# Selective scan and an integer feed-forward in a twelve-layer decoder kernel: buffers that change places from pass to pass, B turned by transposes, delta by halves, and whole-number weights in fp32r

## The chip, the cores and the metric

The kernel runs on one core of one Trainium2 chip. The metric is the time of the device in microseconds (us), the median of several runs. A core has five engines with queues of their own: TensorE (PE in the profile, its weight loads PEld), VectorE (DVE), ScalarE (ACT), GpSimd (POOL) and SyncE (SP, which here only issues transfers). They meet on semaphores alone.

## What is computed

Twelve layers run one after the other on x, 2 sequences of 1024 positions and 256 channels. The change touches two. Layer five is a gated feed-forward whose weights are whole numbers from -127 to 127, times 1/127; xn is x after a norm over its channels:

```python
g, u = xn @ (w_gate.T * SCALE), xn @ (w_up.T * SCALE)      # 256 -> 768, SCALE = 1/127
x = x + (silu(g) * u) @ (w_down.T * SCALE)                 # 768 -> 256
```

Layer six is a selective scan over 512 inner channels and 16 states, run over each sequence forward and backward, and followed by a feed-forward that the change leaves alone:

```python
xc, z = split(xn @ in_proj_w)                 # 512 and 512
u = silu(conv4(xc))                           # causal, four taps
dt, B, C = split(u @ x_proj_w)                # 16, 16, 16
delta = softplus(dt @ dt_proj_w + dt_proj_b)  # 512
h = h * exp(delta * A) + (delta * u) * B      # at each position, 512 x 16 states
y = (sum_n h * C + u * D) * silu(z)
out = y @ out_proj_w
```

## The kernel before, in words

Each engine's program is written out stage by stage (`build`, line 3752). A stage has a method for each engine; marks (`wait_ge`) order the engines, and `Meet` (line 433), or `e.meet` within a stage, makes every engine wait for all that the others have done so far.

**Layer five** (`stages_5`, line 1478). `Dequant` turns the loaded int32 weights, 4608 columns on 128 partitions, into fp32 in place, times 1/127: VectorE two thirds, GpSimd one. `Norm` (line 241) norms 16 tiles of 128 positions on VectorE, TensorE turns them, and ScalarE copies them into `K.XNT`. After a meeting, `Swiglu` (line 1410) goes over four blocks of 512 positions. For each of six chunks of 128 hidden channels TensorE makes the gate product and the up product, two fp32 matmuls of 512 columns each, in banks of PSUM that two chunks share in turn; ScalarE takes silu of the one, VectorE multiplies by the other into `hT`. After a block's chunks TensorE makes the down product of the block before (`down`: six matmuls of 256 columns for each of 16 tiles, 96 in all), and VectorE adds it to x (`summed`), behind the six chunks of the block in its queue.

**Layer six** (`Mamba`, line 2061) makes four passes: sequence 0 and 1 forward, then, after the norm's result has been turned round (`pe_flip`), both backward. A pass has two parts.

*Preparation* (`pe_before`, `pe_delta` and their like on ScalarE and VectorE): TensorE makes the inner channels in four chunks of two halves of 512 positions; ScalarE copies them into `xp` (which lie where the states `h` lie), VectorE runs the convolution with four operations of 1024 columns for each chunk, ScalarE takes silu: `u`. TensorE multiplies `u` by x_proj for dt, B and C as rows ("6 dbc"), and again for B with positions on the partitions ("6 BT", 8 x 4 matmuls of 16 columns). VectorE splits B and C into three bf16 parts (`dve_parts`). TensorE makes delta's product, two halves of four chunks with 16 rows, ScalarE takes abs, exp(-x) and log(1+x), VectorE the maximum and the sum, then `du` = delta * u.

*Scan*: TensorE turns `du` in eight blocks (`pe_turn`), ScalarE copies them out. Then 32 states follow (k: 2 halves of the sequence by 16 states). For each, ScalarE makes a diagonal matrix of B (`Dg`) and exp(delta * A) (`dA`) for four chunks, TensorE the product with B (`pe_dB`) and a copy of C on all partitions (`pe_C`), VectorE four scans of 512 columns (`dve_h`) with two multiplications, GpSimd h * C in two operations, and TensorE sums the result over the states in PSUM (`pe_sum`, matmuls with the identity, three groups behind). Only two buffers exist for `h`, so a state's scan waits for the sum of the second state before it.

*Between two scans*: TensorE makes z for the gate (`pe_gate`, two halves of four chunks), with the last sums between them; VectorE finishes y and multiplies by silu(z); then comes the next preparation, and after delta's product the out product of the pass that ended (`pe_out`, eight tiles of four matmuls of 256 columns), which VectorE copies out ahead of the next delta. In the two backward passes a matmul more for each tile turns it back. `de` and `u` have a buffer each, so the next `u` can't be made before y has been finished. Each pass begins with `e.meet`.

Of the kernel before, what the change touches and what calls it, by code (L numbers as in the profile page):

```python
# [15 lines left out]
S = 1024  # L16
NT = 16
# [6 lines left out]
RRW = 13212  # L24
ENGINES = ("pe", "act", "dve", "pool", "sp")
# [99 lines left out]
class Heap:  # L125
# [5 lines left out]
    def take(self, dims, dt=F32, p0=0, p1=128):  # L131
        n = int(np.prod(dims))
        off = self.at
        self.at += n if dt in (F32, I32) else (n + 1) // 2
# [7 lines left out]
class Kernel:  # L142


    def __init__(self, nc, ctx, ins, out):
        self.nc, self.ctx, self.ins, self.out = nc, ctx, ins, out
        self.AR = ctx.enter_context(nc.sbuf_tensor("AR", [128, LOW], F32))
        with nc.sbuf_tensor("SC", [128, TOT - LOW], F32) as SC:
            self.SC = SC
        self.RR = ctx.enter_context(nc.sbuf_tensor("RR", [128, RRW], F32R))  # L150
# [32 lines left out]
    def view(self, off, dims, dt=F32, p0=0, p1=128):  # L183
        n = int(np.prod(dims))
        words = n if dt in (F32, I32) else n // 2
# [6 lines left out]
        if dt != F32:  # L192
            ap = ap.bitcast(dt)
# [31 lines left out]
class Weights(Stage):  # L225


    def __init__(self, K, heap, name, dt=F32):
        self.n = K.ins[name].shape[1]
        self.to, self.src, self.ready = heap.take([self.n], dt), K.ins[name], K.load(f"d_{name}")  # L230
# [1160 lines left out]
class Dequant(Stage):  # L1391


    def __init__(self, K, w):
        self.K, self.w = K, w

    def dve(self, e):
        wf = self.w.to.bitcast(F32)
        e.wait_ge(self.w.ready, "all")
        for k in (0, 2):  # L1400
            s_ = slice(1536 * k, 1536 * k + 1536)
            e.tensor_scalar(wf[:, s_], self.w.to[:, s_], 1.0 / 127.0, None, ALU.mult).then_inc(self.K.vv, ("dequant", k))

    def pool(self, e):
        s_ = slice(1536, 3072)
        e.wait_ge(self.w.ready, "all")
        e.tensor_scalar(self.w.to.bitcast(F32)[:, s_], self.w.to[:, s_], 1.0 / 127.0, None, ALU.mult).then_inc(self.K.gv, ("dequant", 1))


class Swiglu(Stage):  # L1410


    def __init__(self, K, tag, nf, wg, wu, wd):
        self.K, self.tag, self.nf, self.wg, self.wu, self.wd = K, tag, nf, wg, wu, wd
        self.hT = [K.scr.take([nf, 512]) for _ in range(2)]
        self.sg = [K.scr.take([512]) for _ in range(2)]

    def pe(self, e):
        K, tag, PS, nf = self.K, self.tag, self.K.PS, self.nf

        def down(k):
            e.wait_ge(K.vv, (tag, "h", k, nf - 1))
            for i2 in range(2):
# [3 lines left out]
                for z in range(2):  # L1427
                    i = 2 * i2 + z
                    for f in range(nf):
                        t = e.matmul(PS[:, b, 256 * z:256 * z + 256], self.hT[k % 2][:, f, 128 * i:128 * i + 128], self.wd(f),  # L1430
                                     start=f == 0, stop=f == nf - 1)
                t.then_inc(K.mm, (tag, "down", k, i2))
        for k in range(4):
            for f in range(nf):
# [2503 lines left out]
```

## Time and profile before

| | us |
|---|---|
| median of 3 runs | 6441.59 (6440.6 to 6453.47) |
| the profiled execution | 6446.8, its span 6445.0 |
| TensorE busy | 5578.4, granted clock 0.915 in the mean |
| VectorE, ScalarE, GpSimd busy | 3949.9, 2840.0, 1751.8 |

The rows further down are of this profiled execution. Times are from the start of its span. A granted clock of 1.0 is 2.4 GHz and 0.5 is 1.2 GHz; a mean between them says how long each was granted. A group of the timeline merges instructions of a kind that follow each other: its start, the time from the first's start to the last's end, engine, line, operation, operands, count, and in brackets the idle time before it with what ended it. The line is that of the helper which issues (73 matmul, 76 transpose, 79 activation, 82 tensor with tensor, 85 tensor with scalar, 88 both, 91 scan).

### The profile page before, as it was taken

The numbers are of one execution on the slowest core, as the hardware profiler recorded it, in microseconds if no ns is written. First come the engines' busy times: TensorE is split into PE (matmuls) and PEld (weight loads), VectorE is DVE, ScalarE is ACT, GpSimd is POOL, SyncE is SP. The second block draws the span as 40 slices with busy tenths as digits, with TensorE's granted clock in tenths as the row PEclk, the third lists the DMA queues.
The fourth block names the chain that finished last, engine by engine and source line by source line (L and its number), as shares of the span: only waits on it lengthen the run. The fifth ranks groups of instructions, "written<-read, shape, count | busy, mean of one in ns | idle before, by whom it ended". The sixth has DMA issues, their size and how long they took to land. (4 is left out here: it accounts for less than half of the span.)

```text
span 6445.0 us, 76892 instructions
## 1 busy us (share of the span) xinstructions
PE 5578.4 (87%) x30276; PEld 3058.1 (47%) x30292; DVE 3949.9 (61%) x6870; ACT 2840.0 (44%) x4511; POOL 1751.8 (27%) x1879
## 2 busy tenths in 40 slices
PE   7978999998968889989998989987858878899685
PEld 4434445455444545656555643336734344333354
DVE  5666776766565279787795257751267754788412
ACT  4553444443026156656563246651135545466400
POOL 2302333332032036445463122102132132311112
PEclk9998999998879979898999889988979989799898
DMA  1000000000000000000000010004400000000122
GB/s 50 1 3 1 1 1 1 1 1 20 10 18 1 11 23 1 1 1 1 1 1 1 10 40 1 1 7 166 166 23 1 1 16 13 18 1 1 42 99 85
DMA packets 47910, 135.08 MB, mean 21 GB/s; under 512 B 4822, under 2 KB 31990, under 8 KB 41534
## 3 DMA queue, kind: packets, MB, share of 16 engines
q1 hardware_dynamic: 38094, 77.67, 3.5%
q0 software_dynamic: 9456, 52.50, 2.3%
q8 instruction: 239, 3.92, 0.3%
q14 instruction: 121, 0.99, 0.1%
HBM read 99.42 MB, written 31.20 MB: 20 GB/s over the span
## 5 line engine op out<-in xcount | busy, mean ns | idle before, releaser
L73 PE MATMUL PS<-SC 128*32 128x512 f32 (+13 forms) x14832 | 2807.9, 429 | 137.7 <-ACT SC L79 61.3
L79 ACT ACTIVATE SC<-PS 128x1024 f32<-128x1024 f32 (+9 forms) x2553 | 1932.5, 782 | 2031.0 <-PE PS L73 1676.9
L73 PEld LDWEIGHTS PS<-SC 128*32 128x32 f32 (+7 forms) x14832 | 1211.6, 129 | 1468.9 <-issue 596.7
L94 DVE TENSOR_REDUCE SC<-PS 128x1 f32<-128x512 f32 (+5 forms) x2368 | 1517.1, 681 | 602.3 <-PE PS L73 589.4
L82 POOL TENSOR_TENSOR SC<-SC 128x1024 f32<-128x1024 f32 (+3 forms) x892 | 1189.9, 1344 | 1538.3 <-ACT SC L79 1319.3
L73 PE MATMUL PS<-AR 128*128 128x512 f32 (+8 forms) x4286 | 1222.5, 401 | 70.0 <-DVE SC L82 14.7
L76 PE MATMUL PS<-AR,SC 128*104 128x128 bf16 (+3 forms) x4628 | 534.6, 261 | 499.6 <-DVE SC L85 216.9
L73 PEld LDWEIGHTS PS<-AR 128*128 128x128 f32 (+4 forms) x4286 | 659.0, 178 | 511.7 <-issue 316.3
L73 PE MATMUL PS<-SC,AR 128*128 128x512 f32 (+6 forms) x1922 | 770.6, 527 | 38.5 <-ACT SC L79 13.6
L76 PEld LDWEIGHTS PS<-AR,SC 128*104 128x104 bf16 (+3 forms) x4628 | 415.3, 139 | 714.5 <-issue 414.2
L91 DVE TENSOR_TENSOR_SCAN SC<-SC,PS 128x512 f32<-128x512 f32 x512 | 610.2, 1234 | 3.0 <-ACT SC L79 3.0
L97 POOL CAST SC<-SC 128x256 bf16<-128x256 f32 (+2 forms) x696 | 264.4, 407 | 1203.5 <-DVE SC L82 656.3
L79 ACT ACTIVATE SC<-SC 128x512 f32<-128x512 f32 (+7 forms) x870 | 444.7, 563 | 275.8 <-DVE SC L85 132.1
L73 PE MATMUL PS<-AR,SC 128*128 128x256 f32 (+5 forms) x1856 | 464.3, 402 | 13.3 <-DVE SC L85 10.4
L73 PEld LDWEIGHTS PS<-SC,AR 128*128 128x128 f32 (+4 forms) x1938 | 321.6, 177 | 305.9 <-issue 232.4
L82 DVE TENSOR_TENSOR SC<-SC 128x1024 f32<-128x1024 f32 (+10 forms) x523 | 398.0, 773 | 106.2 <-ACT SC L79 92.6
L73 PE MATMUL PS<-RR 64*128 64x512 f32 (+2 forms) x2688 | 429.7, 441 | 18.8 <-DVE SC L94 18.6
L73 PEld LDWEIGHTS PS<-AR,SC 128*128 128x128 f32 (+2 forms) x1856 | 333.5, 202 | 140.5 <-issue 84.4
L82 DVE TENSOR_TENSOR SC<-PS,SC 128x256 f32<-128x256 f32 (+5 forms) x321 | 142.9, 454 | 401.7 <-PE PS L73 198.7
L97 DVE COPY SC<-PS 2x512 bf16<-2x512 bf16 (+4 forms) x397 | 207.7, 523 | 238.9 <-PE PS L76 129.4
L73 PEld LDWEIGHTS PS<-RR 64*128 64x128 f32 (+1 forms) x2688 | 240.8, 185 | 151.0 <-DVE SC L94 52.0
L79 ACT ACT_TABLE_LOAD x50 | 64.2, 1283 | 532.4 <-DVE SC L85 354.0
(73 smaller groups left out, 1990.9 us busy)
## 6 DMA issues: line engine op xcount, KB each, us to landing
xg<-AR SPq DMA_DIRECT2D x20, 512.0 KB, 5.6
SC<-in_pk11e SPq DMA_DIRECT2D x8, 1152.0 KB, 6.4
SC<-in_pk11e SPq DMA_DIRECT2D x8, 1028.0 KB, 5.1
SC<-xg SPq DMA_DIRECT2D x23, 256.0 KB, 2.9
yg<-SC SPq DMA_DIRECT2D x23, 256.0 KB, 2.2
SC<-xg SPq DMA_DIRECT2D x8, 512.0 KB, 6.1
yg<-SC SPq DMA_DIRECT2D x8, 512.0 KB, 3.3
AR<-in_pk SPq DMA_DIRECT2D x2, 1562.0 KB, 8.6
```

What stands on the lines that cost most here:

```text
L73: return Step(self.real and self.real.matmul(*a, **k))
L76: return Step(self.real and self.real.transpose(*a, **k))
L79: return Step(self.real and self.real.activation(*a, **k))
L82: return Step(self.real and self.real.tensor_tensor(*a, **k))
L91: return Step(self.real and self.real.tensor_tensor_scan(*a, **k))
L94: return Step(self.real and self.real.tensor_reduce(*a, **k))
L97: return Step(self.real and self.real.tensor_copy(*a, **k))
```

## The change

**Layer five.** `Whole` copies the weights as the whole numbers that they are into fp32r (VectorE two thirds, ScalarE one); a view of the same memory is of that type. `NormParts` keeps the turned norm as two fp32r parts, high (ScalarE) and low, what is missing from the high one (VectorE); the meeting behind it is gone. Each product is two fp32r matmuls, high and low. The hidden values are split likewise: VectorE writes the product to `full`, ScalarE the high part, VectorE the low one. 1/127 is applied by silu's scale, in the product and in the sum. `summed` of the block before moves from behind the six chunks to behind the fourth (f == 3).

**Layer six.** `u` and `de` change places from pass to pass (`ud`). `xp` moves to where `dA` lies, and its products to other banks. In passes 0 to 1 and 2 to 3 the next pass's inner channels, convolution and `u` are made ahead of and between the last sums and gates; in 1 to 2 the order stays. ScalarE copies all 64 rows of dt, B and C to `dbl`; VectorE's parts read them from there, and B with positions on the partitions comes from eight transposes of 16 rows of `dbl`. Delta's product runs half, B, half. At the start of a pass delta and `du` of the first half are made and turned first; the second half is turned in front of the first sum (p == 3). The meetings at each pass are gone.

```diff
@@ -1388,38 +1397,70 @@
-class Dequant(Stage):
...
+class NormParts(Norm):
...
+    def turned(self, e):
+        K, tag = self.K, self.tag
+        for k in range(4):
+            for c in range(2):
+                e.wait_ge(K.mm, (tag, "turn", k, c))
+                e.activation(self.hi[:, c, 512 * k:512 * k + 512], K.PS[:, 2 * k + c, :], ACT.Copy).then_inc(K.av, (tag, "hi", k, c))
+
+    def dve(self, e):
+        K, tag = self.K, self.tag
+        super().dve(e)
+        for k in range(4):
+            for c in range(2):
+                s_ = slice(512 * k, 512 * k + 512)
+                e.wait_ge(K.av, (tag, "hi", k, c))
+                e.tensor_tensor(self.lo[:, c, s_], K.PS[:, 2 * k + c, :], self.hi[:, c, s_].bitcast(F32), ALU.subtract).then_inc(K.vv, (tag, "lo", k, c))
...
+            e.tensor_copy(self.to[:, s_], self.w.to[:, s_]).then_inc(self.K.vv, ("whole", k))
...
+        e.activation(self.to[:, s_], self.w.to[:, s_], ACT.Copy).then_inc(self.K.av, ("whole", 1))
...
+            e.wait_ge(K.vv, (tag, "lo", k, nf - 1))
+            if k == 0:
+                e.wait_ge(K.vv, (x.tag, "lo", 3, 1))
...
+                        for p in range(2):
+                            t = e.matmul(PS[:, b, 256 * z:256 * z + 256], self.h[k % 2][p][:, f, 128 * i:128 * i + 128], self.wd(f),
+                                         start=f + p == 0, stop=f == nf - 1 and p == 1)
...
-                        t = e.matmul(PS[:, 2 * y + z, :], w(f, c), K.XNT[:, c, 512 * k:512 * k + 512], start=c == 0, stop=c == 1)
+                        for p, part in enumerate((x.hi, x.lo)):
+                            t = e.matmul(PS[:, 2 * y + z, :], w(f, c), part[:, c, 512 * k:512 * k + 512], start=c + p == 0, stop=c + p == 2)
...
+        def high(n):
+            k, f = divmod(n, nf)
+            if k >= 2:
+                e.wait_ge(K.mm, (tag, "down", k - 2, 1))
+            e.wait_ge(K.vv, (tag, "h", n))
+            e.activation(self.h[k % 2][0][:, f, :], self.full[n % 2], ACT.Copy).then_inc(K.av, (tag, "hi", n))
+        for n in range(4 * nf):
+            y = n % 2
             e.wait_ge(K.mm, (tag, "up", n, 0))
             if n >= 2:
-                e.wait_ge(K.vv, (tag, "h", *divmod(n - 2, self.nf)))
-            e.activation(self.sg[y], K.PS[:, 2 * y, :], ACT.Silu).then_inc(K.av, (tag, "silu", n))
+                e.wait_ge(K.vv, (tag, "h", n - 2))
+            e.activation(self.sg[y], K.PS[:, 2 * (n % nf % 2), :], ACT.Silu, scale=self.unit).then_inc(K.av, (tag, "silu", n))
+            if n > 0:
+                high(n - 1)
+        high(4 * nf - 1)
...
+        def low(n):
+            k, f = divmod(n, nf)
+            e.wait_ge(K.av, (tag, "hi", n))
+            e.tensor_tensor(self.h[k % 2][1][:, f, :], self.full[n % 2], self.h[k % 2][0][:, f, :].bitcast(F32), ALU.subtract).then_inc(K.vv, (tag, "lo", k, f))
+        for n in range(4 * nf):
+            k, f = divmod(n, nf)
+            e.wait_ge(K.mm, (tag, "up", n, 1))
+            e.wait_ge(K.av, (tag, "silu", n))
+            if n >= 2:
+                e.wait_ge(K.vv, (tag, "lo", *divmod(n - 2, nf)))
+            e.scalar_tensor_tensor(out=self.full[n % 2], in0=K.PS[:, 2 * (f % 2) + 1, :], scalar=self.unit, in1=self.sg[n % 2],
+                                   op0=ALU.mult, op1=ALU.mult).then_inc(K.vv, (tag, "h", n))
+            if n > 0:
+                low(n - 1)
+            if k > 0 and f == 3:
                 summed(k - 1)
+        low(4 * nf - 1)
         summed(3)
...
-        self.u, self.de, self.du = take([4, S]), take([4, S]), take([4, S])
+
+        self.ud, self.du = [take([4, S]) for _ in range(2)], take([4, S])
...
-        self.xp = [h.rearrange("p a b -> p (a b)")[:, 0:1027] for h in self.h]
+        self.xp = [a.rearrange("p a b -> p (a b)")[:, 0:1027] for a in self.dA]
...
+    def pe_xp(self, e, sq, c):
+
+
+        K = self.K
+        for half in range(2):
+            if c >= 2:
+                e.wait_ge(K.av, ("6 xp", sq, c - 2, half))
+            elif sq in (1, 3):
+                if c == 0 and half == 0:
+                    e.wait_ge(K.av, ("6 C", sq - 1, 31))
+                else:
+                    e.wait_ge(K.vv, ("6 h", sq - 1, 31, {(0, 1): 1, (1, 0): 2, (1, 1): 3}[c, half]))
+            self.pe_xz(e, sq, c, half, self.xp_bank(c, half)).then_inc(K.mm, ("6 xp", sq, c, half))
...
-            for c in range(4):
-                t = e.matmul(PS[:, 6, 16 * tb:16 * tb + 16], self.u[:, c, 128 * tb:128 * tb + 128], self.xpw[:, c, 32:48], start=c == 0, stop=c == 3)
...
+            t = e.transpose(K.PS[:, 6, 16 * tb:16 * tb + 16], self.dbl[32:48, 128 * tb:128 * tb + 128], K.ident[32:48, 32:48])
...
+    def pe_turn(self, e, sq, half):
+
+        K = self.K
+        e.wait_ge(K.vv, ("6 du", sq, half))
+        if half == 0:
+            e.wait_ge(K.av, ("6 BT", sq))
+        for tb in range(4 * half, 4 * half + 4):
...
-            e.meet(K.marks, ("6 pass", sq))
-            self.pe_turn(e, sq)
...
+                if p == 3:
+                    self.pe_turn(e, sq, 1)
...
+            n = sq + 1
+            if sq in (0, 2):
+                self.pe_xp(e, n, 0)
+                self.pe_last(e, sq, 61)
+                self.pe_xp(e, n, 1)
+                self.pe_last(e, sq, 62)
+                self.pe_last(e, sq, 63)
+                self.pe_xp(e, n, 2)
+                self.pe_xp(e, n, 3)
+                self.pe_gate(e, sq, 0)
+                self.pe_dbc(e, n)
+                self.pe_gate(e, sq, 1, (0, 1))
+                self.pe_dt(e, n, 0)
+                self.pe_gate(e, sq, 1, (2, 3))
+                self.pe_BT(e, n)
+                self.pe_dt(e, n, 1)
+                self.pe_out(e, sq, range(8), self.K.vv)
+                continue
             self.pe_gate(e, sq, 0)
...
-            e.meet(K.marks, ("6 pass", sq))
+            self.act_dA(e, sq, 0)
             self.act_turned(e, sq, 0)
-            self.act_spread(e, sq, 0)
+            self.act_diag(e, sq, 0)
+            self.act_C(e, sq, 0)
+            self.act_spread(e, sq, 1)
             self.act_turned(e, sq, 1)
-            self.act_spread(e, sq, 1)
...
+            if sq in (0, 2):
+                self.act_xp(e, n, 0)
+                self.act_xp(e, n, 1)
+                self.act_xp(e, n, 2)
+                self.act_u(e, n, 0)
+                self.act_xp(e, n, 3)
+                self.act_u(e, n, 1)
+                self.act_u(e, n, 2)
+                self.act_gate(e, sq, 0, (0, 1, 2))
+                self.act_u(e, n, 3)
+                self.act_gate(e, sq, 0, (3,))
+                self.act_dbl(e, n)
+                self.act_gate(e, sq, 1, (0, 1))
+                self.act_abs(e, n, 0)
+                self.act_gate(e, sq, 1, (2, 3))
+                self.act_BT(e, n)
+                self.act_abs(e, n, 1)
+                self.act_log(e, n)
+                continue
...
+            self.dve_du(e, sq, 0)
+            self.dve_delta(e, sq, 1)
             self.dve_du(e, sq, 1)
             for k in range(32):
                 self.dve_h(e, sq, k)
...
+            if sq in (0, 2):
+                self.dve_edges(e, n)
+                self.dve_conv(e, n, 0)
+                self.dve_y(e, sq, 1)
+                for c in range(1, 4):
+                    self.dve_conv(e, n, c)
+                self.dve_gated(e, sq, 0)
+                self.dve_parts(e, n)
+                self.dve_max(e, n, 0)
+                self.dve_gated(e, sq, 1)
+                self.dve_max(e, n, 1)
+                self.dve_out(e, sq, range(8), True)
+                self.dve_delta(e, n, 0)
+                continue
             self.dve_y(e, sq, 1)
```

## Rows read from the trace of the kernel before

**Rows 1.** The page, part 1: busy time and share of each engine.
```profile
PE 5578.4 (87%) x30276; PEld 3058.1 (47%) x30292; DVE 3949.9 (61%) x6870; ACT 2840.0 (44%) x4511; POOL 1751.8 (27%) x1879
```

**Rows 2.** Windows: busy time (count) per engine, then granted clock, DMA share, GB/s.
```profile
2103.70:2125.40 21.70, 8.51 (x32) 6.13 (x32) 19.02 (x58) 6.33 (x13) 4.72 (x1) 0.56 0.14 49
2125.40:2252.60 127.20, 126.34 (x384) 73.75 (x384) 22.15 (x33) 15.61 (x25) 0.00 (x0) 0.98 0.00 0
...
2268.80:2347.00 78.20, 58.18 (x162) 32.23 (x162) 40.58 (x46) 35.23 (x46) 0.00 (x0) 0.64 0.00 0
2347.00:2539.40 192.40, 186.29 (x837) 117.29 (x838) 188.19 (x195) 137.62 (x316) 147.84 (x63) 0.98 0.00 1
2539.40:2638.20 98.80, 87.10 (x269) 50.42 (x267) 51.08 (x63) 38.31 (x52) 2.35 (x1) 0.83 0.00 0
...
2831.80:2951.00 119.20, 96.97 (x332) 59.56 (x331) 64.29 (x117) 46.56 (x66) 2.34 (x1) 0.80 0.00 0
...
3143.50:3246.10 102.60, 90.59 (x285) 53.24 (x283) 54.42 (x70) 38.26 (x52) 2.35 (x1) 0.83 0.00 0
```

**Rows 3.** Groups by form, TensorE in 2125.4 to 2252.6: count, busy, mean ns.
```profile
L73 PE MATMUL PS<-AR 128*128 128x512 f32 x192 | 85.2, 605 | 0.7 <-PE PS L76 0.7
L73 PE MATMUL PS<-AR,SC 128*128 128x256 f32 x192 | 41.9, 379 | 0.0
```

**Rows 4.** Timeline, layer five: the conversion, and VectorE's part of a chunk.
```profile
2103.72 5.74 DVE L85 TENSOR_SCALAR AR<-AR 128x1536 f32<-128x1536 int32 x2
...
2103.93 4.72 POOL L85 TENSOR_SCALAR AR<-AR 128x1536 f32<-128x1536 int32 x1 [67.16 <-DVE AR L82]
2109.38 1.39 DVE L106 BATCH_NORM_STATS2 SC<-AR 128x6 f32<-128x256 f32 x4
...
2131.65 0.69 DVE L82 TENSOR_TENSOR SC<-PS,SC 128x512 f32<-128x512 f32 x1 [8.48 <-PE PS L73]
```

**Rows 5.** Timeline of TensorE in layer one: pairs of fp32r matmuls from RR.
```profile
701.84 1.20 PE L73 MATMUL PS<-RR 64*128 64x512 f32 x8
...
704.35 1.94 PE L73 MATMUL PS<-SC 128*64 128x512 f32 x8
```

**Rows 6.** Timeline of TensorE from the end of scan 0 into scan 1.
```profile
2538.34 7.13 PE L73 MATMUL PS<-AR 128*128 128x512 f32 x16 [0.83 <-DVE SC L91]
...
2583.51 10.29 PE L73 MATMUL PS<-AR,SC 128*128 128x16 f32 x64
2593.73 14.02 PE L73 MATMUL PS<-SC,AR 16*128 16x512 f32 x16
2607.67 15.87 PE L73 MATMUL PS<-AR,SC 128*128 128x256 f32 x64
2630.75 1.94 PE L76 MATMUL PS<-AR,SC 128*128 128x128 f32 x8 [7.21 <-DVE SC L82]
...
2640.92 1.16 PE L73 MATMUL PS<-SC 128*128 128x128 f32 x8 [0.86 <-ACT SC L79]
...
2646.46 3.78 PE L73 MATMUL PS<-SC,AR 128*128 128x512 f32 x4 [0.58 <-POOL SC L82]
```

**Rows 7.** Windows: delta's products, busy times as in rows 2, then granted clock.
```profile
2593.70:2607.60 13.90, 13.90 (x17) 5.16 (x16) 5.25 (x7) 5.09 (x8) 0.00 (x0) 0.50 0.00 0
```

**Rows 8.** Timeline of GpSimd and VectorE from scan 0 into scan 1.
```profile
2539.54 2.35 POOL L82 TENSOR_TENSOR SC<-SC 128x1024 f32<-128x1024 f32 x1 [0.59 <-DVE SC L91]
...
2575.73 0.81 DVE L85 TENSOR_SCALAR SC<-SC,AR 128x1024 f32<-128x1024 f32 x1
...
2576.57 3.93 DVE L88 SCALAR_TENSOR_TENSOR SC<-SC,AR 128x1024 f32<-128x1024 f32 x3
...
2623.92 9.01 DVE L82 TENSOR_TENSOR SC<-SC 128x2048 f32<-128x2048 f32 x4
...
2638.18 2.33 DVE L91 TENSOR_TENSOR_SCAN SC<-SC,PS 128x512 f32<-128x512 f32 x2 [0.97 <-ACT SC L79]
...
2653.25 2.33 DVE L91 TENSOR_TENSOR_SCAN SC<-SC,PS 128x512 f32<-128x512 f32 x2
```

**Rows 9.** Timeline of ScalarE: exp(-x) of delta, both halves.
```profile
2609.78 3.71 ACT L79 ACTIVATE SC<-SC 128x2048 f32<-128x2048 f32 x2
```

More of the change, by code:

```diff
@@ L2143, in pe_delta @@
             for half in range(2):
-                if c == 0 and sq > 0:
-                    e.wait_ge(K.av, ("6 z", sq - 1, 1, half))
-                t = e.matmul(PS[0:64, 4 + half, :], self.xpw[:, c, :], self.u[:, c, self.half(half)], start=c == 0, stop=c == 3)
+                if c == 0:
+                    e.wait_ge(K.av, ("6 xp", sq, 3, half))
+                t = e.matmul(PS[0:64, 4 + half, :], self.xpw[:, c, :], self.u(sq)[:, c, self.half(half)], start=c == 0, stop=c == 3)
                 if c == 3:
@@ L2148, in pe_delta, with pe_dt @@
                     t.then_inc(K.mm, ("6 dbc", sq, half))
-        if sq > 0:
+    def pe_dt(self, e, sq, half):
+        K = self.K
+        e.wait_ge(K.av, ("6 dbl", sq, half))
+        for c in range(4):
+            if half == 1:
+                e.wait_ge(K.vv, ("6 max", sq, 0, c))
+            elif sq in (1, 3):
+                e.wait_ge(K.av, ("6 z", sq - 1, 0, c))
+            elif sq == 2:
+                e.wait_ge(K.vv, ("6 y", 1, 1, c))
+            e.matmul(K.PS[:, c, :], self.dtw[0:16, 128 * c:128 * c + 128], self.dbl[0:16, self.half(half)], start=True,
+                     stop=True).then_inc(K.mm, ("6 dt", sq, half, c))
@@ L2154, in pe_delta @@
         t.then_inc(K.mm, ("6 BT", sq))
-        for half in range(2):
-            for c in range(4):
-                bank = c
-                if half == 1:
-                    e.wait_ge(K.vv, ("6 max", sq, 0, c))
-                else:
-                    e.wait_ge(K.av, ("6 xp", sq, 2 + c // 2, c % 2))
-                e.wait_ge(K.av, ("6 dbl", sq, half))
-                e.matmul(PS[:, bank, :], self.dtw[0:16, 128 * c:128 * c + 128], self.dbl[0:16, self.half(half)], start=True,
-                         stop=True).then_inc(K.mm, ("6 dt", sq, half, c))
@@ L2323, in act_delta, with act_log @@
+    def act_log(self, e, sq):
+        K = self.K
         for half in range(2):
[L2324 to L2328 removed]
+            d = self.de(sq)[:, :, self.half(half)]
             e.wait_ge(K.av, ("6 abs", sq, half, 3))
@@ new lines, in act @@
+            self.act_gate(e, sq, 0)
+            self.act_gate(e, sq, 1)
+            if sq == 1:
+                self.act_flip(e)
+                for c in range(4):
+                    self.act_xp(e, n, c)
+                    if c >= 1:
+                        self.act_u(e, n, c - 1)
+                self.act_u(e, n, 3)
+                self.act_dbl(e, n)
+                self.act_abs(e, n, 0)
+                self.act_BT(e, n)
+                self.act_abs(e, n, 1)
+                self.act_log(e, n)
@@ L2443, in dve_parts @@
             s_ = self.half(half)
-            src = K.PS[32:64, 4 + half, :]
-            e.wait_ge(K.mm, ("6 dbc", sq, half))
+            src = self.dbl[32:64, s_]
+            e.wait_ge(K.av, ("6 dbl", sq, half))
             if half == 1:
@@ L2556, in dve @@
         e.tensor_scalar(self.An, self.An, -1.0, None, ALU.mult).then_inc(K.vv, "6 A")
-        self.dve_before(e, 0)
-        self.dve_delta(e, 0)
-        self.dve_delta_end(e, 0)
+        self.dve_edges(e, 0)
+        for c in range(4):
+            self.dve_conv(e, 0, c)
+        self.dve_parts(e, 0)
+        self.dve_max(e, 0, 0)
+        self.dve_max(e, 0, 1)
+        self.dve_delta(e, 0, 0)
         for sq in range(self.passes):
-            e.meet(K.marks, ("6 pass", sq))
+            self.dve_du(e, sq, 0)
+            self.dve_delta(e, sq, 1)
             self.dve_du(e, sq, 1)
```

348 lines of the change are left out of this document (194 added, 154 removed).

## The prediction

> **What bounds the kernel now.** I read the page first: TensorE is busy 87% of the span, no other engine over 61% [rows 1]. That average hides that layers five and six, which the change touches, have different limits, so I cut 2103.7 to 3476.7 us into stretches by busy time [rows 2]. Layer five is two stretches: a norm of 21.7 us in which VectorE is busy 19.0 and TensorE 8.5, and 127.2 us in which TensorE is busy 126.3. There, only TensorE's work counts. Layer six is a prologue of 78.2 us, four scans of some 192.4 us, and turn-rounds of 98.8, 119.2 and 102.6 us between them. In a scan VectorE and TensorE are both at 97 to 98%; nothing of the change is in the steady loop, so I leave the scans alone. In the turn-rounds TensorE is busy 81 to 88%, at a granted clock of 0.80 to 0.83, VectorE about half: one serial chain, carried mostly by TensorE, partly at its lower clock. The timelines then give the chain step by step [rows 6 to 9].
>
> **Layer five, the matmuls.** The 127.2 us hold 192 records of 512 columns and 192 of 256 [rows 3]; the code issues 96 matmuls of each kind, so an fp32 matmul is two records. Busy time over count is 85.2/192 = 0.44 us and 41.9/192 = 0.218 us a record, a little of it start-up at the low clock; the clean pace is 0.427 and 0.213. The change doubles the matmuls (high part, low part) and makes each fp32r. The nearest rows are layer one's fp32r matmuls, 64 rows by 512 columns, in pairs on the two halves of the array: from 701.84 to 704.35 ten pairs start (eight of fp32r, two of bf16, one record a matmul), 0.251 us a pair [rows 5]. A pair is two matmuls side by side, so one fp32r matmul of 512 columns is one pass: not under 0.213 (half an fp32 record, which is two passes), not over 0.251 if 128 rows behave as 64 do. I take 0.23: 192 x 0.23 = 44.2 us (41 to 48). At 256 columns the stream is 0.107; no row has fp32r there. Eight records of 128 columns, each with its own weight load, took 1.16 us with latency [rows 6], 0.145 at most, so loads can follow each other at about that. I take 0.125: 24 us (20.5 to 28).
>
> A rule of the Trainium skill speaks against this (TensorE: Matmul & The Clock Gate, "The mechanism"): a weight load overlaps running matmuls only when its row group differs. All new matmuls use all rows, so by it each would wait for its load. That rule doesn't fit the fp32 rows, where two loads and 2 x 0.427 us of streaming make 0.853 and no more; it is rival 1.
>
> **Layer five, the waits.** VectorE gets more per hidden chunk: the product and the low part, 0.69 us each [rows 4], 1.4 us against 8 x 0.23 = 1.84 us of up-matmuls; ScalarE two operations of 0.6. They fit, TensorE stays the bound. But VectorE's sum of the block before now stands behind chunk 3, and waits for down-products that TensorE issues only after chunk 5. Chunks 4 and 5 queue behind it. Twice (blocks 1 and 2) TensorE finishes, starts the next block's gate product (0.9 us) and then waits for sum and chunk 4 (0.2+0.69+0.69): 0.8 us lost. In the last block all of sum, chunk 4, low 3, chunk 5, low 4, high 5 and low 5 stand before the last down: 4.7 us. Together 6.3. Low clock at the start costs 2.4 as now (127.2 against 192 x 0.427 + 192 x 0.213 = 123). New stretch: 44.2+24+6.3+2.4 = 77 us, gain **50** (39 to 56).
>
> The conversion: two VectorE operations of 1536 columns took 5.7 us with GpSimd's 4.7 beside them [rows 4]. The third piece goes to ScalarE, idle then. I take 1.25 each without GpSimd (an estimate: 1024 columns take 0.81 [rows 8], so 1536 some 1.2; bounds 1.25 and 2.87): 3.2 us gained (0 to 3.2). The low parts of the norm (0.69 each) let the first matmul start when two are done, about 0.7 earlier than the meeting did. Layer five: 50 + 3.2 + 0.7 = **54 us**.
>
> **Layer six, B and delta.** B's turn was 32 matmuls of 16 columns, 64 records, 10.3 us [rows 6]. Eight transposes replace it; at the low clock a transpose is 0.24 us (eight in 1.94), so 1 to 2 us; I take 1.5. It stands in the chain in all four preparations, between the products and delta. Delta's eight products took 14.0 us, 1.71 each, all at granted clock 0.50 [rows 6, 7]; at the high level they would be 0.85. Before them came B's many short matmuls, during which the clock fell.
>
> Order at the start of a pass: VectorE did delta 0, delta 1, du 0, du 1 in 9.01 us [rows 8], 2.25 each, so du 0 ended at 2630.7. Now du 0 comes second, 2.25 us sooner. But then: from du 0's end the first scan came after 7.5 us, and the third state's (2653.25) after 22.5 [rows 8]; from there on the pace is 5.88 us a state. New: four transposes' copies, diagonal, B product, multiply: first scan after 6.0. Du's second half is turned only after the fourth B product, which needs the first scans; ScalarE's four copies for it stand ahead of the copies of the last states, for which GpSimd waits, and the y sums wait for GpSimd. Worked through with the rows' durations: TensorE turns at 13.3, ScalarE done at 15.8, GpSimd 16.2 to 18.6 (2.35 an operation [rows 8]), sum of state 0 at 22.0 (low clock; 3.78 for two, [rows 6]), C, B product (2.5), multiply: third scan at 25.3; at the high clock 22.8. I take 24.8. So 2.25 is gained and 2.3 to 3.4 lost: the halves bring nothing by themselves, -0.3 to -1.
>
> **Prologue.** B saves 10.0. Delta's first half starts at the high level and gains 3.4; the second waits for VectorE's split of B and C (6 us), loses about 1.5: 11.7, less 1.2 at the start of the pass: **10.5** (8 to 15).
>
> **Pass 1 to 2** (the flip stays where it is): B 8 to 9; delta products between 0 and 5 better; the start of the pass -1: **9.5** (6 to 14).
>
> **Passes 0 to 1 and 2 to 3.** Here the next pass's products, its convolution and u move ahead of the gates and sums, since u and delta change places. The convolution (4 x 4.7 us of VectorE; three of the four operations are 3.93 [rows 8]) kept TensorE nearly idle before its last products; now gates fill that. So I add up TensorE's work from the last scan's end: it comes free 1.9 us before it, at 2537.5 (2538.34 less 0.83 idle): next x 13.7 (16 records are 7.1 with latency, 6.8 without [rows 6]), three sums 5.1, gates 13.7, dbc 6.8, delta 6.8, B 1.0 to 1.5, out 13.8: 61, end at 59. Checked against VectorE: last convolution at 25.5, last u at 26.6, needed at 28.5: 2 us of slack. ScalarE's exponential and logarithm (3.71 and about 3.9, a table load of 1.28 before each [rows 9]) end by 56, so the out product is last; then copy 0.4, delta 0 and du 0, 4.5: du 0 at 64.4 against 91.2 now (2539.45 to 2630.7). For the clock falling at the short products I add 3.5: 68. Third scan at 68+24.8 = 92.8 against 113.8: **21**, and 20.7 for 2 to 3 (17 to 26 each). Removing the meetings is contained in this: the waits that remain are on buffers.
>
> Sum: 10.5+21+9.5+20.7 = 62 in layer six (50 to 78), 54 in layer five, **116 us**. The profiled execution took 6446.8 (span 6445.0); 6331. The median of the runs is 5.2 lower: **6326**.
>
> **Rivals.** (1) Loads exposed on full rows. For: no row shows fp32r with 128 rows, and pairs ran at 0.251 rather than 0.213. Against: fp32 hides its loads. A load is about 0.107 (half of a 256-column record): 192 x 0.32 + 192 x 0.214 = 102.5 instead of 68, 34 more: 6360. The Trainium skill's rule named above would give this.
> (2) fp32r on 128 rows runs at an fp32 record's pace, 0.427 and 0.213: 123 instead of 68, and the stalls stay. Layer five gains nothing: 6381. Against: pairs of 64 rows don't show it.
> (3) The turn-rounds give less: transposes and 16-row products pull the clock down, and gates and out run slow, 6 us in each of four places: 24 more, 6350. For: during delta's products the clock stood at 0.50, and eight full transposes took 1.94 us, low-level pace [rows 6, 7]. The Trainium skill (TensorE: Matmul & The Clock Gate, "PE-mode transpose") says that the full clock doesn't engage for transposes; the trace's transposes agree. Against: four products are now followed by dense gates.
> (4) Slower: fp32r on full rows takes four passes as fp32 does, in layer five's up and down loops, 0.853 and 0.427: 192 x 1.28 = 246 instead of 68, 178 more: 6504. It decides from 0.95 us for the two together. Against: the 0.251 of a pair.
> The convolution's 2 us of slack being gone is contained in (3).
>
> **Chances.** Forecast 0.52 (own range 6300 to 6345), (1) 0.13, (2) 0.09, (3) 0.22, (4) 0.03, both gains lost 0.01. The range reaches to (3) and (1): 6298 to 6370, leaving out (2), (4) and a little below. A measurement can tell 0.2% (13 us) from nothing. Faster 0.96, within 0.01, slower 0.03.
>
> **What would show it.** Layer five's TensorE stretch: one record a matmul, 192 of each width, spaced 0.23 and 0.125, in 77 us; idle of 0.8, 0.8 and 4.7 us behind VectorE. No 64-record group of 16 columns. From last scan to first scan 74 us instead of 98.8 (0 to 1), about 78 (2 to 3); the step to the third state longer than 8.3 us, behind GpSimd. If records are 0.427 apart, (2); if the gates run at half clock, (3). What would make it wrong at once: a wait of TensorE on VectorE in the middle of the turn-round.

## The result, and the profile after

The changed kernel takes 6334.59 us (median of 4 runs, 6333.54 to 6335.71), the kernel before 6444.14 (4 runs beside them, 6440.6 to 6453.47). The ratio is 0.9832, with a 95% interval of 0.982 to 0.9844: 1.7% faster. The forecast was 6326, 8.6 us too low and inside the range of 6298 to 6370. About 5 of the 8.6 is in the sum of the gains, which is 111.1 us of span (6445.0 less 6333.9) instead of 116. The rest is my step from the profiled execution to the median, since the profiled execution of after (6335.7) stands 1.1 above its median, not 5.2.

The page, part 1, of the kernel after. It answers to [rows 1]: TensorE has lost 107 us of busy time, 208 matmul records net, and the other engines little.

```profile
PE 5471.7 (86%) x30068; PEld 3002.4 (47%) x30068; DVE 3959.9 (63%) x6902; ACT 2852.2 (45%) x4536; POOL 1745.4 (28%) x1878
```

Windows of the kernel after, columns as in [rows 2]: conversion and norm of layer five, its matmuls, the prologue of layer six, then the turn-rounds 0 to 1, 1 to 2, 2 to 3.

```profile
2104.00:2122.00 18.00, 8.56 (x35) 6.20 (x33) 17.20 (x62) 7.22 (x13) 0.00 (x0) 0.60 0.17 59
2122.00:2199.90 77.90, 72.11 (x385) 61.94 (x384) 39.58 (x62) 29.39 (x50) 0.00 (x0) 0.94 0.00 1
2216.00:2278.40 62.40, 40.51 (x96) 17.59 (x97) 39.80 (x46) 37.94 (x53) 0.00 (x0) 0.72 0.00 0
2475.40:2548.50 73.10, 67.03 (x199) 35.66 (x198) 50.42 (x60) 41.12 (x59) 2.36 (x1) 0.93 0.00 0
2742.40:2850.80 108.40, 86.43 (x264) 49.78 (x264) 63.56 (x117) 49.40 (x73) 2.34 (x1) 0.80 0.00 0
3046.20:3128.20 82.00, 75.75 (x215) 40.94 (x214) 53.84 (x71) 41.16 (x59) 2.36 (x1) 0.88 0.00 1
```

Against [rows 2], layer five's matmuls take 77.9 us instead of 127.2, at the same number of records. The turn-rounds take 73.1, 108.4 and 82.0 instead of 98.8, 119.2 and 102.6, and in the first and the third the granted clock is up from 0.83 to 0.93 and 0.88. In the middle one, which is not mixed, it stayed at 0.80.

I cut both executions at the same events: start of the conversion, start of the norm that ends layer five, end of a pass's last scan, first scan of the third state of the next. From there to its last scan a pass took 178.5 us in every kernel of this study.

| part, us saved | forecast | measured |
|---|---|---|
| layer five | 54 | 54.0 |
| layer six, prologue | 10.5 | 11.4 |
| turn-round 0 to 1 | 21 | 25.3 |
| turn-round 1 to 2 | 9.5 | 7.9 |
| turn-round 2 to 3 | 20.7 | 17.0 |
| outside these parts | 0 | -4.5 |
| sum | 116 | 111.1 |

Of the -4.5, 1.3 lie ahead of layer five and 3.2 behind the last scan of layer six.

In layer five, the timeline of TensorE in the kernel after (columns: start, duration, engine and operation, count, idle before it with what released it):

```profile
2121.96 23.82 PE L74 MATMUL PS<-QB,QA 128*128 128x512 f32 x96
2145.62 5.84 PE L74 MATMUL PS<-QA,QB 128*128 128x256 f32 x48
2151.30 1.09 PE L74 MATMUL PS<-QB,QA 128*128 128x512 f32 x4
2152.84 10.53 PE L74 MATMUL PS<-QB,QA 128*128 128x512 f32 x44 [0.45 <-DVE SC L89]
...
2180.81 5.84 PE L74 MATMUL PS<-QA,QB 128*128 128x256 f32 x48
2190.81 8.37 PE L74 MATMUL PS<-QA,QB 128*128 128x256 f32 x48 [4.16 <-DVE QB L83]
```

An fp32r matmul is one record, 48 of 256 columns pass in 5.84 us, and TensorE waits for VectorE where the prediction said so: 0.45 after the next block's gate product (twice), 4.16 before the last down-products. After that wait the same 48 records need 8.37 us, at a granted clock of 0.68.

In the turn-round 0 to 1, the timeline of TensorE in the kernel after, against [rows 6]:

```profile
2485.28 13.90 PE L74 MATMUL PS<-AR 128*128 128x512 f32 x32
2499.11 7.08 PE L74 MATMUL PS<-SC,AR 128*64 128x512 f32 x16
2506.12 3.70 PE L74 MATMUL PS<-AR 128*128 128x512 f32 x8
2509.75 3.69 PE L74 MATMUL PS<-SC,AR 16*128 16x512 f32 x8
2513.38 5.40 PE L74 MATMUL PS<-AR 128*128 128x512 f32 x8
...
2519.52 3.16 PE L74 MATMUL PS<-SC,AR 16*128 16x512 f32 x7
2522.61 14.08 PE L74 MATMUL PS<-AR,SC 128*128 128x256 f32 x64
2541.73 1.97 PE L77 MATMUL PS<-AR,SC 128*128 128x128 f32 x8 [5.04 <-DVE SC L83]
```

No wait is left from the last sums to the end of the out product, the next pass's last products and the gates (the 32 records of 512 from AR, half of them each, and twice 8 more of gates) fill the time of the convolution, and delta's 16 records (3.69 and about 3.9 us) run near 0.45 us each instead of 0.88. B's eight transposes, and the first of delta's second eight records, lie in the 0.8 us left out between 2518.71 and 2519.52.

### The profile page after: what moved, and what is told of

It is laid out like the page before. It is cut to its first block and busy times, and to the rows that moved or that the text cites. A ratio compares the mean times of both kernels' runs of the same rounds, so it can differ in the third digit from the quotient of the medians.

```text
span 6333.9 us, 76568 instructions
## 1 busy us (share of the span) xinstructions
PE 5471.7 (86%) x30068; PEld 3002.4 (47%) x30068; DVE 3959.9 (63%) x6902; ACT 2852.2 (45%) x4536; POOL 1745.4 (28%) x1878
## 5 line engine op out<-in xcount | busy, mean ns | idle before, releaser
L74 PE MATMUL PS<-AR 128*128 128x128 f32 (+6 forms) x4094 | 1145.9, 393 | 68.5 <-DVE SC L83 14.8
L77 PE MATMUL PS<-AR,SC 128*104 128x128 bf16 (+2 forms) x4660 | 534.7, 260 | 485.3 <-DVE SC L86 213.1
L74 PEld LDWEIGHTS PS<-AR 128*128 128x128 f32 (+2 forms) x4094 | 624.7, 178 | 468.7 <-issue 276.3
L74 PE MATMUL PS<-SC,AR 128*128 128x512 f32 (+7 forms) x1938 | 755.4, 513 | 48.0 <-DVE SC L83 13.3
L77 PEld LDWEIGHTS PS<-AR,SC 128*104 128x104 bf16 (+2 forms) x4660 | 415.8, 138 | 700.8 <-issue 372.9
L74 PE MATMUL PS<-AR,SC 128*128 128x256 f32 (+4 forms) x1408 | 378.0, 419 | 13.3 <-DVE SC L86 10.4
L83 DVE TENSOR_TENSOR SC<-PS,SC 128x256 f32<-128x256 f32 (+3 forms) x289 | 120.7, 427 | 330.5 <-ACT SC L80 191.0
L74 PEld LDWEIGHTS PS<-AR,SC 128*128 128x128 f32 (+2 forms) x1408 | 254.5, 192 | 128.8 <-issue 79.4
```

What stands on the lines that cost most here:

```text
L74: return Step(self.real and self.real.matmul(*a, **k))
L77: return Step(self.real and self.real.transpose(*a, **k))
L83: return Step(self.real and self.real.tensor_tensor(*a, **k))
```

## The experiments

All are edits of the kernel after, but for l5_alone, which has only layer five's part of the change, and l6_alone, which has only layer six's. Numbers in brackets are 95% intervals of the ratio to the kernel before; for the kernel after it is 0.9832 (0.982 to 0.9844).

### The two halves of the change

```diff
 (l5_alone)  class Mamba: of the kernel before; Dequant, Swiglu, stages of layer five: of after
 (l6_alone)  class Mamba: of the kernel after; Dequant, Swiglu, stages of layer five: of before
```

(The classes that allot the memory are those of after in both.)

> The kernel before with layer five's change alone. My theory: the gains of the two layers are independent, and layer five's is what TensorE saves in its own stretch: 148.9 us (2103.72 to 2252.59) become 95, with up products 0.233 us apart and down products 0.12, so 54 us less than before, some 6390, while layer six stays as in before (78, 98.8, 119.2, 102.6 between scans). Rival: part of the 111 us comes or goes elsewhere (the changed kernel's layers outside five and six together are 4.5 us longer than in the profile before): then this one's time differs from before by less than 50 or more than 58 us although its layer five takes 95.

> The changed kernel with layer five as before. My theory: layer six alone gives 61 to 62 us (11.4, 25.3, 7.9 and 17.0 from the end of the scan or norm before to the third state of each pass): 6382. Rival: with layer five as before, the clock or the memory traffic at the start of layer six is another, and the prologue gives less than 8 or more than 15 us; or the sum of this gain and layer five's is not that of the changed kernel, by over 5 us.

Measured: l5_alone 6393.76 us, 0.9924 (0.9907 to 0.994); l6_alone 6392.52, 0.9918 (0.9901 to 0.9934). In l5_alone layer five took 93.05 us against 148.86, a little better than the 94.87 in after. In l6_alone the parts of layer six came out as in after, to 0.5 us (prologue to the third scan 97.4 against 96.9, turn-rounds 88.5, 125.4 and 100.5). So neither half needs the other for its gain. But unchanged code didn't keep its time: in l5_alone, whose layer six is that of before, the turn-rounds to the third state took 112.4, 137.3 and 116.5 us against 113.8, 133.2 and 117.5, so the middle one alone was 4.0 longer. And l6_alone's time missed its expectation by 10 us, and these lie behind layer six, where its instructions are those of both other kernels: from the last scan on it took 3015.7 us, before 3005.5, after 3008.7. By the medians the two halves gave 51.5 and 52.8 us, 104.3 together, where the whole change gave 109.6: 5.3 short, just past the 5 us that I had named as the rival's sign. The profile puts most of the difference behind layer six (3015.7 against 3008.7 us), not into the layers that were changed. One place of this kind, TensorE in the layer after six, first the kernel after, then the kernel before:

```profile
3388.42 30.64 PE L74 MATMUL PS<-AR 128*128 128x512 f32 x64 [10.83 <-POOL AR L83]
```

```profile
3502.76 29.12 PE L73 MATMUL PS<-AR 128*128 128x512 f32 x64 [10.65 <-POOL AR L82]
```

The same 64 records after nearly the same wait take 1.5 us more, at a granted clock of 0.90 against 0.95 in the windows of these two stretches. From the last scan to the end the kernels of this study took 3002.8 to 3015.7 us, and they came to the start of layer five between 2101.9 and 2110.1 us; I can't predict the sign of either. The -4.5 of the table is of this kind.

### The order of the turn-rounds

```diff
-            if sq in (0, 2):        # xp, u and convolution ahead of gates and sums (PE, ACT, DVE)
+            if False:
...
-            if sq == 1:
-                self.pe_flip(e)
+            if sq < 3:
+                if sq == 1:
+                    self.pe_flip(e)
```

(The waits on buffers, and the gates' banks, follow the order of 1 to 2.)

> The changed kernel without the mixing in passes 0 to 1 and 2 to 3: gates and sums first, then the next preparation, as in 1 to 2; transposes, changed buffers and delta by halves stay. My theory: the serial chain comes back, in which TensorE idles during the convolution. From the last scan to du's first half: 91.2 before, less 9.3 for B's turn, 2.3 for the order of du, 0 to 5 for a better clock: 75 to 80 against 66 in the changed kernel, so 9 to 14 us more in each of the two, 6353 to 6362. Rival: the mixing is worth little because TensorE's work alone fills the time; less than 4 us each, 6342 or less. Then the gain of 25 and 17 us would be that of the transposes and the clock.

Measured: 6356.14 us, 0.9862 (0.9843 to 0.9882), 21.6 over the kernel after, inside the expected 6353 to 6362. Its two parts were not inside theirs, 9 to 14 each: the turn-round 0 to 1 took 16.2 us more to the third state, 2 to 3 took 5.0 more. That the sum fits is in part luck. To the first scan they took 13.0 and 8.2 us more; the step from the second state to the third then added 3.2 in the one and took back 3.2 in the other. TensorE in 0 to 1, last scan at 2472.2:

```profile
2490.97 14.00 PE L74 MATMUL PS<-AR 128*128 128x512 f32 x32 [0.69 <-ACT SC L80]
2506.59 3.62 PE L74 MATMUL PS<-SC,AR 128*64 128x512 f32 x8 [1.62 <-ACT SC L80]
...
2515.38 4.27 PE L74 MATMUL PS<-SC,AR 128*64 128x512 f32 x9 [2.75 <-ACT SC L80]
...
2523.55 7.19 PE L74 MATMUL PS<-SC,AR 16*128 16x512 f32 x8 [2.60 <-DVE SC L86]
2530.66 15.94 PE L74 MATMUL PS<-AR,SC 128*128 128x256 f32 x64
```

The waits are back (0.69, 1.62, 0.49, 2.75 and 2.60 us of them), and the eight second delta products behind the last of them run at 0.90 us each, for 7.19 us, where the mixed order has 0.45. Mixing gives both the filled waits and a good part of the clock.

### B's turn

```diff
         for tb in range(8):
-            t = e.transpose(K.PS[:, 6, 16 * tb:16 * tb + 16], self.dbl[32:48, 128 * tb:128 * tb + 128], K.ident[32:48, 32:48])
+            for c in range(4):
+                t = e.matmul(K.PS[:, 6, 16 * tb:16 * tb + 16], self.u(sq)[:, c, 128 * tb:128 * tb + 128], self.xpw[:, c, 32:48], start=c == 0, stop=c == 3)
```

> The changed kernel with B's turn made again by 32 matmuls of 16 columns in place of eight transposes, at the same place. My theory: it stands in TensorE's chain in all four preparations and each pays 7 us (64 records 0.11 apart at the full clock) to 10 (at the half), less about 1.0 for the transposes: 6 to 9 each, 24 to 37 in all, 6359 to 6372. Rival 1: in the mixed preparations it hides behind ScalarE or VectorE: only two of the four pay, 12 to 18 us, 6347 to 6353. Rival 2: its short products also pull the clock down for what follows (delta's second half 1.71 apart rather than 0.85, the first out tiles slow): 5 us more for each, 45 us and more.

Measured: 6389.07 us, 0.9914 (0.9894 to 0.9933), 54.5 over the kernel after. My expectation fell and the rival's held. To the third state the four preparations took 10.8, 19.8, 15.4 and 11.8 us more: 57.8. Timeline of TensorE in 0 to 1, then windows of the same stretches (the last figure but two is the granted clock):

```profile
2521.07 6.71 PE L74 MATMUL PS<-AR 128*128 128x512 f32 x8
2527.62 10.97 PE L74 MATMUL PS<-AR,SC 128*128 128x16 f32 x64
2538.53 7.19 PE L74 MATMUL PS<-SC,AR 16*128 16x512 f32 x8
2545.65 16.74 PE L74 MATMUL PS<-AR,SC 128*128 128x256 f32 x64
```

```profile
2527.60:2538.50 10.90, 10.90 (x65) 10.86 (x63) 0.69 (x1) 0.60 (x1) 0.00 (x0) 0.64 0.00 0
2538.50:2545.60 7.10, 7.10 (x9) 2.50 (x8) 2.25 (x3) 2.34 (x4) 0.00 (x0) 0.50 0.00 0
2545.60:2562.30 16.70, 16.70 (x65) 13.97 (x64) 3.72 (x8) 12.14 (x8) 0.00 (x0) 0.84 0.00 1
```

The first scan came 18.3 us later than in after. From the start of B's turn to the out product took 18.0 us instead of 3.9 (2527.62 to 2545.65, in after 2518.71 to 2522.61), 14.1 more. Behind B's products delta's eight second records took 7.19, where 8 at 0.45 are 3.6, and the out product 16.74 instead of 14.08: some 6 us of low clock, granted 0.50 and 0.84. The rest, 10 to 11, is the time of B's products themselves. The other 1.6 of the 18.3 came before B's turn (gate 6.71 instead of 5.40, delta's first half 4.03 instead of 3.69), and isn't B's doing. So B's turn cost about 17 us here, of which the prediction named 10 as its own time and counted the clock under "delta".

### The second half of delta * u

```diff
-                if p == 3:
+                if p == 0:
                     self.pe_turn(e, sq, 1)
...
-            self.act_spread(e, sq, 1)
             self.act_turned(e, sq, 1)
+            self.act_spread(e, sq, 1)
```

> The changed kernel with du's second half turned right after the first B product of the first state (TensorE p == 0 instead of 3), and ScalarE's four copies of it ahead of the second state's work instead of behind it. My theory: in the changed kernel these copies stand in ScalarE's queue until TensorE's turn at 13 us after du's first half, the copies of the last states wait behind them, GpSimd starts at 15.9 us and the third state's scan at 22.2 (full clock, pass 1) to 25.4 (half clock, pass 3). With the turn at once GpSimd starts at 12.3 and the step from the second to the third state falls from 12.9, 9.7, 11.2, 12.9 us to 6 to 9: 3 to 5 us in each pass, 12 to 20 in all, 6315 to 6323. Rival: the third state is late because TensorE runs at half clock after its pause and has the turns to do as well, wherever they stand; then the step stays within 1.5 us and so does the time, 6329 or more.

Measured: 6323.91 us, 0.9815 (0.9799 to 0.9831), 10.7 under the kernel after. From the second state to the third took 8.9, 9.0, 9.4 and 8.9 us in the four passes, where after had 12.9, 9.7, 11.2 and 12.9. The differences add up to 10.5, and layer six as a whole is 10.7 shorter. My 3 to 5 us in each pass came in the first and the last only, and the time missed the expected 6315 to 6323 by a little. The gain of 10.7 is that of the medians; two of the four runs took 6318 and two 6329, and the profiled one, of 6318.2, is another 6.8 shorter outside layer six. What made the step long is seen in the fourth pass of the kernel after, GpSimd and TensorE:

```profile
3138.04 4.65 POOL L83 TENSOR_TENSOR SC<-SC 128x1024 f32<-128x1024 f32 x2 [89.41 <-ACT SC L80]
```

```profile
3135.47 1.91 PE L77 MATMUL PS<-AR,SC 128*128 128x128 f32 x8
3140.44 3.78 PE L74 MATMUL PS<-SC,AR 128*128 128x512 f32 x4 [3.05 <-POOL SC L83]
```

TensorE turns the second half at 3135.47, ScalarE copies it, GpSimd starts behind that copy, and TensorE waits 3.05 us for GpSimd. With the turn ahead, that wait is 0.26 us in the same pass (in the second pass 0.34, where after has 3.23). The edit moved the turn and its copies together, so it doesn't part their shares. In 0 to 1, however, turn_at_once had its first scan 3.3 us later than after: the same second delta products and out product took 4.61 and 15.97 us instead of 3.16 and 14.08, at clocks of 0.72 and 0.88 instead of 1.00. The instructions up to there, and their spacing, are the same in both.

### The sum of the block before, in layer five

```diff
-            if k > 0 and f == 3:
+            if k == 3 and f == nf - 1:
+                low(n)
+            if k > 0 and f == nf - 1:
                 summed(k - 1)
-        low(4 * nf - 1)
         summed(3)
```

> The changed kernel with layer five's sum of the block before behind the sixth chunk instead of the fourth, and in the last block behind the last low part too. My theory: TensorE's two waits of 0.45 us and the one of 4.2 us (2186.6 to 2190.8) vanish, and with them the dip of the clock that follows: 5 to 6.5 us, 6328 to 6330; the sum itself hides beside products. Rival: another wait takes its place, for TensorE needs both sums' banks or the last low part later: less than 2 us.

Measured: 6322.12 us, 0.9807 (0.9791 to 0.9823). That is 12.5 us under the kernel after, where I had expected 5 to 6.5 for the waits and the low clock behind them. Layer five took 86.55 us instead of 94.87, 8.3 less. TensorE:

```profile
2150.63 5.84 PE L74 MATMUL PS<-QA,QB 128*128 128x256 f32 x48
2156.31 11.36 PE L74 MATMUL PS<-QB,QA 128*128 128x512 f32 x48
2167.51 5.85 PE L74 MATMUL PS<-QA,QB 128*128 128x256 f32 x48
2173.20 11.36 PE L74 MATMUL PS<-QB,QA 128*128 128x512 f32 x48
2184.39 11.52 PE L74 MATMUL PS<-QA,QB 128*128 128x256 f32 x96
```

All three waits (0.45, 0.45, 4.16) are gone, and so is the low clock behind the last: the final 96 records take 11.52 us, as much as two groups of 48 at full pace, where after spent 5.84 + 4.16 + 8.37. From this view the paces are clean: 11.20/48 = 0.233 us for 512 columns, 5.68/48 = 0.118 for 256. The other 4 us under the kernel after I can't place: the profiled execution, 6327.53, is the slowest of the four, and its span is only 8.2 below that of after. Outside layer five it was 5.1 us later at the start of that layer, and 2.1 and 2.9 shorter in the prologue and behind the last scan. Behind six chunks is where the kernel before had its sum, so at least the two waits of 0.45 us had come in with the change, which moved it to the fourth; the last low part ahead of the sum is new.

### The meetings put back

```diff
         for sq in range(self.passes):
+            e.meet(K.marks, ("6 pass", sq))      # on all four engines
```

> The changed kernel with the meeting of all engines at the start of each pass put back, everything else as changed. My theory: what ends last before a pass is delta's first half on VectorE, which all others need anyway, and the meeting adds nothing that is not waited for: within 1 us a pass, 6335 to 6339. Rival: the missing barrier is a part of the gain (ScalarE's first exp(delta * A) and GpSimd run ahead): 2 us or more a pass, 6343 or more.

Measured: 6335.57 us, 0.9829 (0.9813 to 0.9846): no difference from the kernel after. Its parts did move: the prologue took 2.9 us less, the turn-round 0 to 1 5.2 more, 2 to 3 5.4 less, and the time behind the last scan was 5.9 longer. In layer six as a whole that is 2.9 less with the meetings, so no cost of theirs shows beside shifts of this size. What the change gains at a pass comes from order and buffers.

### Both improvements together

The edits of turn_at_once and sum_last in one kernel.

> Both edits on the changed kernel: the turn at once and the sum last. My theory: they are 4000 instructions apart and add up: 17 to 26 us less than the changed kernel, 6309 to 6318. Rival: one of them does nothing; then 6315 or 6330, as its single run shows.

Measured: 6314.1 us (6306.75 to 6314.52), 0.9793 (0.9777 to 0.9809). It is faster than both kernels: 130 us under before, and 20.5 under after, its interval wholly below that of after. The two single gains, 10.7 and 12.5, would make 23.2; 20.5 is within the 17 to 26 expected.

## Why the prediction was right, and where a size was off

The mechanisms were right, and layer five's size with them. That the sum of layer six came within 1 us (61.6 against 61.7) is partly luck: 0 to 1 gave 4.3 us more than forecast and 2 to 3 gave 3.7 less. Layer five's 54.0 holds an error each way too, 0.9 us more in the matmuls and 0.9 less before them.

**Layer five, the matmuls.** Right, and for the reason given: one pass and one record for an fp32r matmul on 128 rows. Forecast 0.23 and 0.125, measured 0.233 and 0.118: 67.5 us for 192 of each, against 68.2. Rivals 1, 2 and 4 all ask for other paces (0.32 and 0.214; 0.427 and 0.213; 0.853 and 0.427), and all fall on this. The Trainium skill (TensorE: Matmul & The Clock Gate, "The mechanism") has a rule by which loads on equal rows would be exposed, though the same section also lets a load go ahead into the background weight buffer, which my reading left out. Here 192 loads and 192 products of 256 columns on the same 128 rows pass at 0.118 us a pair, 0.011 over the 0.107 of the stream, so the rule by itself doesn't hold for these.

**Layer five, the waits.** Place and cause right: behind VectorE's sum of the block before. The sizes were 0.45, 0.45 and 4.16 against 0.8, 0.8 and 4.7. What I left out is that the clock falls over the last wait: 48 records in 8.37 us instead of 5.84, 2.5 us more, at 0.68 granted (in l5_alone, behind the same wait, 7.46 at 0.78). The 2.4 for the low clock at the start doesn't follow from its own working, since 127.2 less 123 is 4.2; it measured some 1.3 (23.82 for 96 records, 22.4 by the pace). The stretch was 77.9 against 77.

**The conversion.** Forecast 1.25 us an operation on VectorE; measured 1.83 for two:

```profile
2105.07 1.83 DVE L98 CAST QA<-AR 128x1536 fp32r<-128x1536 int32 x2
```

From the conversion's start to the first matmul 16.9 us instead of 21.7, a gain of 4.8 against 3.9.

**B's turn.** Forecast 1.5 us for the eight transposes, measured 0.8 in the mixed order and 1.03 at low clock in 1 to 2. The saving of 8 to 10 that I set for its own time holds (10 to 11 in 0 to 1). The prediction took the falling clock as something that may or may not come with it ("between 0 and 5 better"); b_by_products makes it 6 us in 0 to 1. That 1 to 2 gave 7.9 and not 9.5 may come from the idle between the products (1.62, 0.49 and 2.75 us), behind which delta's records stay at 0.87 us in after without B's short matmuls too; but this turn-round moved by 4.0 us in l5_alone with no edit of its own, so 1.6 us need no cause of their own:

```profile
2805.98 7.03 PE L74 MATMUL PS<-SC,AR 128*64 128x512 f32 x9 [2.75 <-ACT SC L80]
...
2812.81 9.59 PE L74 MATMUL PS<-SC,AR 16*128 16x512 f32 x11
```

**Turn-rounds 0 to 1 and 2 to 3.** The method, TensorE's work added up from the last scan, was right for 0 to 1: the turn of the first half, which stands right behind du 0, began at 66.3 us (2541.73 less 2475.4), forecast 68 with 3.5 for the clock. From there to the third state took 22.1 (scan at 2563.84), where I took 24.8 and had 22.8 as the value at full clock. Hence 25.3 instead of 21. (Two of my sums were off by little: 59, 0.4 and 4.5 make 63.9, not 64.4, and the prologue's 10.0 + 3.4 - 1.5 is 11.9, not 11.7.) For 2 to 3 the same two numbers were 75.2 and 25.3: the cold value. Both turn-rounds have the same code, but for 16 records more of the out product in the latter, 3.5 us, which before has too. The other 5.4 of the 8.9 between them is nearly all clock. TensorE in 2 to 3:

```profile
3080.57 4.12 PE L74 MATMUL PS<-SC,AR 16*128 16x512 f32 x8
3084.62 6.62 PE L74 MATMUL PS<-AR 128*128 128x512 f32 x8
...
3091.99 4.23 PE L74 MATMUL PS<-SC,AR 16*128 16x512 f32 x7
3096.15 5.99 PE L74 MATMUL PS<-AR,SC 128*128 128x256 f32 x16
```

Against 3.69, 5.40 and 3.16 in 0 to 1, and 3.6 for 16 records of the out product there (14.08/64 each, and latency), that is 0.4 + 1.2 + 1.1 + 2.4 = 5.1 us. So Rival 3 was right in what happens (the clock falls at the products of 16 rows, and the gate and out products behind them run slow; no run took these products out to show that they are the cause) but not in its size: 5 us more in one of two equal turn-rounds, not 6 in each of four places. I had given both 3.5 for it, too much for the one and too little for the other: from last scan to first scan 73.1 and 82.0 us, forecast 74 and about 78. The 2 us of slack at the convolution held: TensorE has no wait there.

**Halves.** "The halves bring nothing by themselves" stands on its working alone, as no run takes the halves out; the working fits step by step: second turn 13.9 us after the first (forecast 13.3 from du 0), GpSimd at 15.8 (16.2), the first state's sum done at 20.1 in 0 to 1 and at 22.8 in 2 to 3 (22.0). From the start of the first turn to the third state took 22.1 and 25.3 us, where before had 22.5. The step from the second state to the third is longer than the 8.3 us that before had in 0 and 2 (9.4 and 9.2 in 1 and 3): 12.9, 9.7, 11.2 and 12.9. That this loss hangs on the late second turn and its copies is what turn_at_once shows.

**Meetings.** Counted at nothing, and nothing shows for them.

**Outside the change** I had counted nothing, and it was 4.5 us. Such shifts in unchanged code (4.0 us in one turn-round, 13 us behind the last scan) can be as large as a medium-sized edit.

## What to carry to other kernels

Where a stage is one serial chain through TensorE, add up TensorE's own work from the last point where it was full, check each other engine's due time against it, and then price every wait twice: the wait, and the slower matmuls behind it (here 4.16 us of wait cost 2.5 us more in one kernel and 1.6 in another). Work of another block put into such waits gives both back. When an operation is moved ahead in a queue, ask who stands behind it: two moves of a few lines (the sum behind the next block's chunks, the second turn ahead of the products) gave 20.5 us more than the change had.

## What the runs showed of the hardware

**The clock falls without any wait.** In the windows of the kernel after, TensorE is busy all the time, and yet its granted clock drops behind the first eight products of 16 rows and comes back:

```profile
2509.70:2513.30 3.60, 3.60 (x9) 1.40 (x8) 3.28 (x6) 2.64 (x4) 0.00 (x0) 1.00 0.00 0
2513.40:2518.70 5.30, 5.30 (x9) 1.98 (x8) 3.34 (x5) 1.28 (x2) 0.00 (x0) 0.68 0.00 0
2518.70:2522.60 3.90, 3.90 (x17) 1.68 (x16) 2.21 (x4) 2.93 (x5) 0.00 (x0) 1.00 0.00 0
```

How long it stays low differs between kernels that issue the same instructions at the same spacing there: 1.00 in the last of these stretches, 0.72 in turn_at_once. What sets that is open, and so is whether the few rows are the cause; no run varied either alone.

**Transposes at the full clock.** Eight transposes of 128 columns take 1.04 us at granted 1.00 in mid-stream and 1.97 at 0.50 behind a wait of 5 us (shown above at 2541.73); the timeline's row for the first, then the windows of both:

```profile
2555.62 1.04 PE L77 MATMUL PS<-AR,SC 128*128 128x128 f32 x8
```

```profile
2555.60:2556.60 1.00, 1.00 (x9) 0.80 (x7) 1.00 (x2) 0.56 (x3) 0.00 (x0) 1.00 0.00 0
2541.70:2543.70 2.00, 1.97 (x8) 1.57 (x8) 2.00 (x1) 1.40 (x4) 0.00 (x0) 0.50 0.00 0
```

The kernel after also has 32 transposes in a row, in a later layer and behind a wait of 6.41 us. They began at the low clock and ended at the full one, with nothing but transposes on TensorE:

```profile
4206.54 6.12 PE L77 MATMUL PS<-AR,SC 128*128 128x128 f32 x32 [6.41 <-DVE SC L86]
```

```profile
4206.50:4210.00 3.50, 3.46 (x16) 3.13 (x17) 2.93 (x14) 3.36 (x18) 0.00 (x0) 0.50 0.00 0
4210.20:4212.70 2.50, 2.46 (x17) 1.63 (x15) 1.60 (x7) 2.50 (x5) 0.00 (x0) 1.00 0.00 0
```

The Trainium skill (TensorE: Matmul & The Clock Gate, "PE-mode transpose") says that the full clock doesn't engage for transposes. That isn't so here: the eight keep the full clock of the matmuls before them, and the 32 gain it by themselves. The row with which I had the rule agree [rows 6] was one behind a wait of 7.21 us, and "the trace's transposes agree" was too wide a reading: in the kernel before, too, 32 in a row behind dense matmuls took 3.66 us at a granted clock of 1.00 (from 3680.90).
